# Turning the gathered embedding rows of a DLRM tower a whole tile at a time, with five transposes and four stores

## What is computed

```python
e = jnp.stack([tbl_0[ids[:, 0]], ..., tbl_38[ids[:, 38]]], axis=1)     # (2048, 39, 16)
z0 = jnp.einsum('bid,bjd->bdij', x0, x0).reshape(B, D, F0 * F0)
cur0 = relu(jnp.einsum('bdk,kl->bld', z0, W0))                           # L = 128
next_h, direct0 = jnp.split(cur0, 2, axis=1)                             # 64 and 64
z1 = jnp.einsum('bid,bjd->bdij', x0, next_h).reshape(B, D, F0 * 64)
cur1 = relu(jnp.einsum('bdk,kl->bld', z1, W1))
z = jnp.sum(jnp.concatenate([direct0, cur1], axis=1), axis=-1)           # (2048, 192)
h = relu(concat([z, dense_ctx]) @ W_top1 + b_top1); h = relu(h @ W_top2 + b_top2); y = h @ W_top3
```

## Time and profile before

| | us |
|---|---|
| median of 3 runs | 1513.18 (1512.98 to 1514.53) |
| the profiled execution, whole | 1513.26 |
| its span, first to last instruction | 1511.5 |
| PE busy | 1442.2 (95%) |
| DVE busy | 1384.0 (92%) |
| POOL busy | 971.7 (64%) |
| ACT busy | 822.5 (54%) |

### The profile page before, as it was taken

How to read it: one execution, slowest core, us unless ns; L and a number is a source line. 1 busy time by engine, 2 the same in 40 slices (tenths; PEclk the granted TensorE clock), 3 DMA queues, 4 the chain that set the end, 5 groups by cost and what they waited for, 6 DMA issues and landing times.

```text
span 1511.5 us, 14915 instructions
## 1 busy us (share of the span) xinstructions
PE 1442.2 (95%) x4458; PEld 785.7 (52%) x4458; DVE 1384.0 (92%) x1244; ACT 822.5 (54%) x897; POOL 971.7 (64%) x604
## 2 busy tenths in 40 slices
PE   4888999999999999999999999999999999999999
PEld 3444545555555554555555555555555555545556
DVE  6778999999999999998999999999999989999993
ACT  1535655655456555545665654556565555655555
POOL 7888888888888778686877868686886830000000
PEclk8999999999999999999999999999999999999999
DMA  5867779888787888877788887878898786778610
GB/s 150 200 154 199 203 190 214 211 186 209 188 205 188 213 198 202 211 184 197 193 199 203 212 204 181 207 190 197 201 207 209 181 207 192 191 194 202 174 35 1
DMA packets 130717, 282.67 MB, mean 187 GB/s; under 512 B 36468, under 2 KB 61700, under 8 KB 130508
## 3 DMA queue, kind: packets, MB, share of 16 engines
q1 hardware_dynamic: 96070, 268.06, 70.4%
q0 software_dynamic: 19200, 4.95, 3.1%
q10 hardware_dynamic: 15366, 8.70, 2.3%
HBM read 273.67 MB, written 7.87 MB: 186 GB/s over the span
## 4 chain that ended last, share of the span: by engine, by line
PE 51%; DVE 26%; issue 14%; POOL 4%; ACT 3%; ACTq 2%; DVEq 0%; DMA 0%
PE psB L533 22%; DVE z L953 12%; PE psA L533 9%; DVE z_lo L962 8%; DVE z_split L953 6%; PE psB L570 4%; PE psB L563 4%; POOL emb L512 4%; PE psB L566 3%; ACTq L751 2%; PE psB L541 1%; ACT z_hi L816 1%; PE psA L553 1%; DVE feat_c L1018 1%; PE psA L563 1%
## 5 line engine op out<-in xcount | busy, mean ns | idle before, releaser
L512 POOL DMA_INDIRECT emb<-in_tbl,ids_all x600 | 971.5, 1619 | 254.5 <-issue 180.1
L533 PE MATMUL psB<-z,w 128*128 128x512 f32 x1544 | 694.0, 594 | 4.1 <-DVE z L953 4.1
L816 ACT ACTIVATE z_hi<-z_split 128x1024 fp32r<-128x1024 f32 x286 | 300.4, 1057 | 465.6 <-DVE z_split L953 410.0
L533 PEld LDWEIGHTS psB<-z,w 128*128 128x128 f32 x1544 | 292.2, 190 | 355.1 <-issue 331.6
L953 DVE TENSOR_TENSOR z<-h_quad,x_lay 128x1024 f32<-128x1024 f32 x354 | 420.2, 1216 | 9.9 <-PE psB L533 4.1
L962 DVE TENSOR_TENSOR z_lo<-z_split,z_hi 128x1024 fp32r<-128x1024 f32 x286 | 349.4, 1222 | 57.7 <-ACT z_hi L816 56.5
L953 DVE TENSOR_TENSOR z_split<-h_quad,x_lay 128x1024 f32<-128x1024 f32 x222 | 267.5, 1217 | 1.7 <-ACT h_quad L769 1.7
L769 ACT ACTIVATE h_quad<-psA 32x1024 f32<-32x1024 f32 x248 | 251.4, 1014 | 3.7
L533 PE MATMUL psA<-z,w 128*128 128x512 f32 x512 | 240.4, 592 | 0.7 <-DVE z L953 0.7
L563 PE MATMUL psB<-z_hi,w_hi 128*128 128x512 f32 x444 | 156.6, 434 | 18.0 <-ACT z_hi L816 18.0
L570 PE MATMUL psB<-z_lo,w_hi 128*128 128x512 f32 x444 | 144.6, 407 | 19.1 <-DVE z_lo L962 17.2
(11 more groups left out here) (121 smaller groups left out, 836.7 us busy)
## 6 DMA issues: line engine op xcount, KB each, us to landing
x_lay<-x_rows SPq DMA_DIRECT2D x1152, 128.0 KB, 7.0
bases<-x_rows SPq DMA_DIRECT2D x62, 468.0 KB
x_more<-x_rows SPq DMA_DIRECT2D x62, 468.0 KB
x_lay<-x_rows SPq DMA_DIRECT2D x64, 256.0 KB, 3.9
x_ring<-x_rows SPq DMA_DIRECT2D x31, 468.0 KB
emb<-in_tbl,ids_all POOLq DMA_INDIRECT x600
x_last<-x_rows SPq DMA_DIRECT2D x64, 128.0 KB, 9.7
x_rows<-x_side ACTq DMA_DIRECT2D x58, 120.0 KB
```

Of the source, the lines that this page charges most:

```text
L512: nc.gpsimd.indirect_dma_start(emb[t % 2][:, f * D:(f + 1) * D], None, tables[f], bass.IndirectOffsetOnAxis(ids_all[:, t, f:f + 1], 0)).th ...
L533: mm = nc.tensor.matmul(ps[:, cs], w[0:k, :], z[WHOLE_NO[place] % NZ][0:k, cs], start=first, stop=last)
L816: nc.scalar.activation(z_hi[n % NS][0:k, 0:cols], z_split[n % NS][0:k, 0:cols], ACT.Copy).then_inc(z_hi_made, 1)
```

## The change

A whole tile is turned straight from `emb`. A row of `emb` holds (f, d) with d running fastest, so 128 neighbouring columns are eight fields; `turn_tile` turns four such pieces and one of 112 columns (the last seven fields) into 640 columns of psA, where a partition is (f, d) and a column is b. `keep_tile` copies them to `x_side` (128 x 512 and 112 x 128), and `store_tile` writes them with four stores into `x_tiles`, which has a row of 8 KB for a field with both units of the tile: two stores write the 39 fields, two write the first 21 again. The spread copies and `emb_spread` are gone. There is one turn a tile: before step 2 of body u for u = 2 to 28 (before step 9 in body 0), kept at step 4 (11). The turn and keep before steps 11 and 13 (15 and 17) are gone. POOL's gather of tile t waits for the turn of tile t - 2. PE, which has no spread to wait for now, waits for the gather itself. Loads read the same 4 KB runs as before, now 8 KB apart.

At the start tile 0 is turned once, after the first two of unit 0's own turns; DVE's copies for unit 0 read `emb[0]` with a step of 16 floats from field to field; ACT appends the first 21 fields behind the 39 in `emb[0]` (`x_wrapped`). SP stores tile 0 and tile 1, ACT the rest.

```diff
-    return ((u + 2, 9), (u + 3, 15)) if u == 0 else ((u + 2, 2), (u + 3, 11))
+    return 9 if u == 0 else 2
...
+        x_turn = half(psA, 0)[:, 0:TURNS * P]
...
+        def store_tile(engine, t):
+            for col, cols, rows, row in ((0, 4, P, 0), (4, 1, LAST_TURN, 4 * DH), (0, 2, P, F), (2, 1, (RING - F - 2 * DH) * D, F + 2 * DH)):
+                x = x_tiles[t, row:row + 1, 0:P]
+                dst = bass.AP(x.tensor, x.offset, [[P, rows], [DH * 2 * C, cols], [1, P]])
+                src = x_side[0:rows, col * P:(col + cols) * P].rearrange("p (q b) -> p q b", b=P)
+                engine.dma_start(dst, src).then_inc(x_stored, 16)
...
-                    pool.wait_ge(spread, 2 * t - 2)
+                    pool.wait_ge(x_turned, t - 1)
+                if t == 2:
+                    pool.wait_ge(part_spread, 7)
...
-                pe.wait_ge(spread, u + 1)
-                if u >= 2:
-                    pe.wait_ge(relu0_done, u // 2 * 2 - 1)
-                for q in range(PAIRS):
-                    pair = emb_spread[:, 2 * q:2 * q + 2, :].rearrange("p d g -> p (d g)")
-                    last = nc.tensor.transpose(turned(u)[0:2 * RING, q * P:(q + 1) * P], pair, ident[:, :])
+                pe.wait_ge(gathered[t % 2], gathered_tile(t))
+                if t < HOT_TILES:
+                    pe.wait_ge(hot_kept, hot_no(t + 1, 0))
+                if t >= 1:
+                    pe.wait_ge(relu0_done, 2 * t - 1)
+                for q in range(TURNS):
+                    rows = P if q < TURNS - 1 else LAST_TURN
+                    last = nc.tensor.transpose(x_turn[0:rows, q * P:(q + 1) * P], emb[t % 2][:, q * P:q * P + rows], ident[:, :])
...
-                nc.scalar.activation(x_side[:, :], turned(u)[0:2 * RING, :], ACT.Copy).then_inc(x_kept, 1)
-                if u >= 3:
-                    act.wait_ge(x_kept, u + 1)
-                    for n in range(2):
-                        act.dma_start(stored(u, n), side(n)).then_inc(x_stored, 16)
+                cols = (TURNS - 1) * P
+                nc.scalar.activation(x_side[:, 0:cols], x_turn[:, 0:cols], ACT.Copy)
+                nc.scalar.activation(x_side[0:LAST_TURN, cols:], x_turn[0:LAST_TURN, cols:], ACT.Copy).then_inc(x_kept, 1)
+                if t >= 2:
+                    act.wait_ge(x_kept, t + 1)
+                    store_tile(act, t)
...
+                x = emb[0][:, first * D:first * D + 1]
+                return bass.AP(x.tensor, x.offset, [list(x.ap[0]), [1, DH]] + [[step * D, count] for step, count in pattern])
```

More of the change, by code:

```diff
@@ L31 @@
 RING = 60
-PAIRS = DH // 2
+TURNS = -(-F * D // P)
+LAST_TURN = F * D - (TURNS - 1) * P
+STORES = 4
 FQ = 9
@@ L214, in tower @@
         left_b = sb_loop("left_b", [P, BANK])
-        emb = [sb_loop(f"emb{n}", [P, F * D]) for n in range(2)]
-        emb_spread = sb_loop("emb_spread", [P, DH, RING])
+        emb = [sb_loop(f"emb{n}", [P, (F, RING)[n == 0] * D]) for n in range(2)]
         h_quad = [[sb_loop(f"h_quad{n}_{k}", [P, C]) for k in range(2)] for n in range(2)]
@@ L299, in tower @@
         gathered = [sem(f"gathered{n}") for n in range(2)]
-        spread = sem("spread")
+        x_wrapped = sem("x_wrapped")
         hot_ids_loaded = [sem(f"hot_ids_loaded{t}") for t in range(HOT_TILES)]
@@ L356, in hot_out, with gathered_tile @@
             return ps[:, first:first + HOT_COL[q + 1] - HOT_COL[q]]
-        def stored(u, n):
-            return x_rows[u, :, :].rearrange("g (q n b) -> n g q b", n=2, b=P)[n]
-        def side(n):
-            return x_side[n * RING:(n + 1) * RING, :].rearrange("g (q b) -> g q b", b=P)
+        def gathered_tile(t):
+            return 16 * sum(gathers(n) for n in range(t % 2, t + 1, 2))
+        def store_tile(engine, t):
[4 more added lines that the diff above has]
+                engine.dma_start(dst, src).then_inc(x_stored, 16)
         block = ctx.enter_context(nc.Block())
@@ L575, in step0 @@
                 last = s == STEPS0 - 2 and not left_units(u)
-                if first:
-                    pe.wait_ge(x_kept, u + len(left_units(u)))
+                if first and u % 2 == 0:
+                    pe.wait_ge(x_kept, u // 2 + 1)
                 if s == STEPS0 - 1:
@@ L636, in turn_part @@
                 last.then_inc(part_turned, 1)
-            turn_x(0)
-            for n in range(6):
+            for n in range(2):
+                turn_part(n)
+            turn_tile(0)
+            for n in range(2, 6):
                 turn_part(n)
@@ L647, in _ @@
             pe.wait_ge(part_kept, 6)
-            turn_x(1)
             for s in range(4, STEPS0):
@@ L728, in _, with keep_tile @@
         def _(act):
[L729 to L751 removed]
+            def keep_tile(t):
+                act.wait_ge(x_turned, t + 1)
+                if t >= 1:
+                    act.wait_ge(x_stored, 16 * STORES * t)
+                cols = (TURNS - 1) * P
[4 more added lines that the diff above has]
+                    store_tile(act, t)
             def relu0(u):
@@ L819, in body @@
                 for s in range(STEPS1):
-                    for v, t in turns(u):
-                        if s == t - (2 if v % 2 == 0 else 1):
-                            spread_x(v)
-                        if s == t + 2:
-                            keep_x(v)
+                    if turn_step(u) is not None and s == turn_step(u) + 2:
+                        keep_tile(u // 2 + 1)
                     if s in split1(u):
@@ L860, in keep_left @@
                 op.then_inc(part_kept, 1)
-            spread_x(0)
-            keep_x(0)
+            act.wait_ge(gathered[0], gathered_tile(0))
+            act.wait_ge(hot_kept, hot_no(1, 0))
+            nc.scalar.activation(emb[0][:, F * D:RING * D], emb[0][:, 0:(RING - F) * D], ACT.Copy).then_inc(x_wrapped, 1)
             keep_part(0, base[0], half(psA, 1))
+            keep_tile(0)
             keep_part(2, base[1], half(psB, 1))
```

92 lines of the change are left out of this document (31 added, 61 removed).

## The result

Four executions of the changed kernel took 1461.60 to 1469.10 us, median 1464.83; the kernel before took 1512.98 to 1514.53, median 1513.54. The ratio is 0.9679 [0.9652, 0.9707]: 49 us less, with the forecast at 1464. The profiled execution is the 1461.60 one, span 1459.8 us; against the profiled one of before the span is 51.7 us shorter. Timed again beside the last experiments, it took 1463.44, 1464.54 and 1466.72 us, ratio 0.9682 [0.9663, 0.9702]; a fourth execution of that series, in the slow state, took 2986.32 us and is left out.

The account below looks back on a forecast made before the run. PE and DVE, both nearly full, were taken to lose time to one stall, DVE's wait for ACT's z_hi at step 13. From 1513.2 us, 42 for the loop and 7 for the start gave 1464; range 1452 to 1485.

Parts of the forecast that it names:

- What bounds the kernel: Loop: PE and DVE both nearly full; idle time comes from DVE's 3.17 us wait for ACT's z_hi at step 13.
- Part 1: Loop: the turn before step 11, its spread, copy and stores go; 3.0 us per two units, 14 times, 42 us.
- Its lower end: Loop: PE wins at least its marked idle time, 0.87 + 0.61 + 0.52 = 2.0 us per two units.
- Part 2: Turn before step 2 gets heavier, four issues taken as 3.0 us; costs 0 until they exceed about 4.8 us.
- requested units ahead: Loop: loads behind SP's wait for the tile's stores are asked for early enough that DVE waits for none.
- Part 3: Start: ACT no longer waits for tile 1's gather, but tile 2's gather, in at 160 us, then binds; gain 7 us.
- PE was free at 80.7: Body 0: without the 5.75 us wait for z_hi, PE reaches the turn at 84.9 us; gain 8.4 us.
- Unit 0's copies: Start: DVE's copies reading every 16th float, -1.2 to +2.5 us for five large ones; taken as 0.
- A: ACT's four stores take 5 to 8 us to issue, delaying step 7's z_hi; 1495 us at 7 us; chance 0.12.
- B: Loop: DVE's freed time doesn't reach PE, gaps only move, 1.5 us per two units stay; 1485 us; chance 0.09.
- C: Start: no wait for tile 2, as POOL runs faster; 1457 us, inside the forecast's range; forecast and C 0.65 and 0.08.
- D: Loads and stores with rows 8 KB apart take longer per packet, DMA engines become the bound; 1572 us; chance 0.06.

Follow-up runs that it names:

- the old kernel with both edits: Kernel before, with odd units' copy and two stores moved from step 13 to step 15 and rows of x 8 KB apart; 1473.10 us, ratio 0.9730.
- the added copies: Changed kernel with three, six or twelve extra 128x512 ACT copies behind each tile's four stores, from tile 2 on; 1465.53, 1480.64 and 1535.17 us.
- the kernel with the moved loads: Changed kernel with SP loading unit 1's x_ring and x_more before unit 0's x_lay 2, 3 and 4; 1461.83 us, ratio 0.9656.
- the turn ahead of step 5: The kernel with the moved loads, with tile 2 alone turned ahead of step 5 of unit 2 rather than step 2; 1462.84 us, ratio 0.9666.

## Why the prediction was right, step by step

- **What bounds the kernel: right.** "The idle time has one source", the stall at step 13. Taking away that delay alone, without the fewer transposes, gave 2.7 of 3.0 us per period.
- **Part 1, 3.0 us per two units, 42 us: right.** Measured 3.01 us (87.49 - 84.48), and 42.3 us from tile 2 to the end. Its inner split is borne out too: 2.7 for the stall, where the old kernel with both edits gained 2.73 for 2.8 us of stall gone, and 0.3 for three fewer transposes, where the chain shows 0.33 and the periods 0.28. Its lower end, the 2.0 us that PE's marks show, was no real bound: in the added copies stall and time agree to 0.1 us, so the stall's value stood near DVE's end, 3.17.
- **Part 2, cost zero: right, with one size off.** The four issues take 2.23 us in the rows above and 1.96 to 3.09 in the fourteen tiles (up to 3.60 in the second profile), where I took 3.0; I priced them in proportion to pieces, from a row (862 ns) that the old layout had made slow, as the kernel with the 8 KB pitch shows (404 ns). The limit that it gave, 4.8 us for the four, was good: 2.23 + 2.73 = 4.96, and the kernels with three, six and twelve copies lie on both sides of it. Loads "requested units ahead" held for this place of the turn and for no other that was tried.
- **Part 3, the start, 7 us: about right as a sum, wrong in its terms.** Body 0 gave 4.9 us, not 8.4. The step of the working that failed is "PE was free at 80.7": it let PE keep its old times up to the gather. Body 0 ran later. DVE waited for x_ring in the kernel before too, to 64.01 us. Now it waited to 64.91 us, although SP issued that load at 55.63 us rather than at 58.13; why it took longer to land is not shown. PE idled for 2.75 us there rather than 0.70, and the run behind it took 3.78 us for four matmuls where 1.88 is usual (granted clock 0.50 from 66 to 70 us, where the kernel before had 1.00). Ten microseconds further on PE was 3.7 us behind the kernel before (75.73 and 71.99 us for the same products); the sum had put nothing there. And 84.9 was out of reach in most executions anyway: the sum had tile 1's gather in at 83 to 84 us, its own row has 84.39, and in four other profiled executions PE waited for it until 86.5 to 87.3 us. From body 0's turn PE took 71.3 us to tile 2's, where it had taken 76.1: 4.9 less, the 3.1 of the sum and what it had called the slow clock of that place. The sum didn't suffer, because it ran through tile 2's gather: that landed at 160.1 as forecast (160), and PE, though late from body 0, was there at 159.7. What did differ is the last term: having waited only 0.38 us, PE lost none of the 2.5 us at low clock that I had deducted, so the gain is 169.47 - 160.10 = 9.4 in the profiled run. The median of the four executions lies 3.2 us above that run, which the sum had no term for; 1464.83 hits 1464 partly for that reason. Had PE come sooner, the 2.5 us would have been due: the kernel with the moved loads lost 2.6.
- **Unit 0's copies, taken as 0: right.** DVE's copies of 936 elements took 0.65 us, as they had from the dense tile. In the first (L1140) each element is read three times in a row, so only every third read moves on; in those of L1144 every element lies at least 64 bytes from the one before. The Trainium skill (SBUF — State Buffer, Door 1: The DMA port swizzle) has lines of 16 bytes and a price for each crossing; these copies cross one at every element and took 646 ns where the dense ones took 644, so the measurement decides against that rule for DVE's long copies. Some of the short ones took a little longer (128x144: 0.28 us after 0.24), too little to see in the time. DVE began 1.0 us sooner, not 1.2.
- **Rivals.** A (dear issues) has the right mechanism, shown by the added copies, and didn't occur: the longest four issues took 3.09 us in one profile and 3.60 in the other, under the limit of 4.8. B (DVE's time doesn't reach PE) is refuted, since it reaches PE in full. C (no wait for tile 2) didn't occur: tile 2's gathers took POOL 73.7 us from first to last issue after 72.2. D (the 8 KB step slows transfers) has the wrong sign: the pitch alone makes the kernel before 14 us faster, although x_lay lands 0.4 us later. The prediction had not seen that the layout sets the price of the issues. In the changed kernel the pitch and the better place can't be told apart by these runs.

## What to carry to other kernels

Before a step is made lighter, look at what stands behind it in its engine's queue: here 2.7 of the 3.0 us per period came from getting 2.4 us of copy and store issues out from in front of one rounding, and a copy of the old kernel with nothing but a moved store and another row pitch gets 40 of the 49 us. The place of a step has three sides, when its input is there, how long its engine is idle behind it, and who waits for what it releases; moving the same turn from step 2 to step 9 met the first two and lost 82 us on the third. In a bracket of idle time see first whether DMA issues lie inside, since they are not counted as busy.

## What the runs showed of the hardware

- The time that an engine needs to issue a DMA depends on the layout in DRAM: 240 pieces of 512 bytes took 853 to 862 ns with rows 4 KB apart and 322 to 404 ns with rows 8 KB apart (minimum and median), from the same SBUF tile on the same queue; SP's own went from a median of 902 to one of 398 ns. The loads' rows moved with the stores', so that it is the stores' own layout is likely, not isolated. Single issues still take up to 1.6 us in the changed kernel.
- A strided read (64 bytes from element to element) cost DVE's fp32 copy of 936 elements nothing: 646 ns, and 644 from the dense tile. Of 144 elements it took 0.28 us rather than 0.24, of 112 it took 0.25 rather than 0.22.
- After PE had stood for 6.06 us, the first five pairs of matmuls at 128x512 took 1.05 to 1.20 us in place of 0.61 to 0.71, with a granted clock of 0.63 over the 7.6 us; in the same place after 3.08 us of idle time (the changed kernel again) they took 0.61 to 0.71, and after 3.76 us (three added copies) the granted clock was 0.80 over the 7 us behind. After 3.15 us in body 0 (the turn ahead of step 5) the first two pairs took 1.20 and 1.05: the length of the idle time alone doesn't decide.
- The last gather of tile 2 landed at 160.1 to 163.4 us in six executions with the same gathers ahead of it, 4.0 to 6.4 us behind the end of its issue. That end lay between 153.7 and 157.1 us, since single issues take POOL between 0.94 and 1.97 us, in a mix that differs from execution to execution.
